# The prologue of a cross-attention and mixture-of-experts kernel: loads and constants in another order, keys ahead of queries, both first normalizations on VectorE

## The reference

```python
x = x + attention(layernorm(x), ctx)      # x, ctx: (8, 256, 256) f32
    q = layernorm(x) @ Wq + bq            # 16 heads of depth 16
    k, v = ctx @ Wk + bk, ctx @ Wv + bv
    attn = softmax(q @ k^T / 4 + mask * -1e9)   # mask: (8, 1, 1, 256)
    out = concat(attn @ v) @ Wo + bo
x = x + moe(layernorm(x))                 # 8 experts, top 2 of softmax(x @ w_gate),
                                          # capacity 1024, silu(a) * g @ c_proj
```

## Time and profile before

| what | value |
|---|---|
| runs | 487.96, 491.83, 487.74 us; median 487.96 |
| profiled execution | 487.79 us, its span 486.0 us |
| mean granted TensorE clock | 0.917 of full speed |
| busy: PE, DVE, POOL, ACT | 80%, 54%, 37%, 35% of the span |
| first row maximum on TensorE | 34.75 us after the span's start |
| start of the experts' steady part | about 300 us |

### The profile page before, as it was taken

How to read it: one execution, slowest core, us unless ns; L and a number is a source line. 1 busy time by engine, 2 the same in 40 slices (tenths; PEclk the granted TensorE clock), 3 DMA queues, 4 the chain that set the end, 5 groups by cost and what they waited for, 6 DMA issues and landing times.

```text
span 486.0 us, 8302 instructions
## 1 busy us (share of the span) xinstructions
PE 389.5 (80%) x2218; PEld 257.8 (53%) x2219; DVE 262.5 (54%) x684; ACT 171.9 (35%) x336; POOL 177.6 (37%) x179
## 2 busy tenths in 40 slices
PE   0647798996969979695868799679999999999970
PEld 0524455664645656453535466457666566656640
DVE  3638566686987969688687546223323232323220
ACT  1430638463654726453354252112221212121210
POOL 5542333322743717352213315213323232323231
PEclk9977889898988989798898689889999999999996
DMA  7499194938749193580405513533232333233420
GB/s 230 152 196 147 38 207 159 207 115 161 213 120 227 50 185 112 128 160 33 140 10 179 187 42 77 109 77 40 51 58 36 60 43 57 43 57 44 61 44 4
DMA packets 65430, 51.75 MB, mean 106 GB/s; under 512 B 11880, under 2 KB 62328, under 8 KB 65400
## 3 DMA queue, kind: packets, MB, share of 16 engines
q1 hardware_dynamic: 57224, 42.36, 38.0%
q0 software_dynamic: 7008, 8.43, 10.3%
q10 hardware_dynamic: 1168, 0.59, 0.5%
HBM read 32.89 MB, written 19.06 MB: 107 GB/s over the span
## 4 chain that ended last, share of the span: by engine, by line
DMA 31%; DVE 25%; PE 24%; issue 10%; SPq 4%; ACT 2%; POOL 1%; ACTq 1%; POOLq 1%; DVEq 0%
DMA out<-CTt,GG 26%; DVE NEG L1043 7%; PE bank L803 5%; PE bank L769 4%; PE bank L868 3%; PE bank L839 3%; PE bank L852 2%; PE bank L776 2%; DVE bn L1001 2%; PE bank L918 2%; DVE AVT L1062 2%; DMA wf<-qparts_d 1%; DVE AVN L1065 1%; DVE ON L1070 1%; DVE R L1079 1%
## 5 line engine op out<-in xcount | busy, mean ns | idle before, releaser
L918 PE MATMUL bank<-wf,XN 128*128 x304 | 108.1, 498 | 1.6 <-DVE CTt L1268 1.0
L571 POOL DMA_INDIRECT out<-CTt,GG x38 | 58.9, 1551 | 133.5 <-DMA out<-CTt,GG 108.5
L1043 DVE TENSOR_REDUCE NEG<-bank 128x2 f32<-128x512 f32 x128 | 83.4, 682 | 42.0 <-PE bank L839 41.2
L670 ACT ACTIVATE PR<-bank 128x512 f32<-128x512 f32 x128 | 73.0, 593 | 80.1 <-PE bank L852 68.6
L918 PEld LDWEIGHTS bank<-wf,XN 128*128 128x128 f32 x304 | 55.5, 194 | 34.7 <-issue 8.2
L839 PE MATMUL bank<-KS,wf 99*128 99x256 bf16 x256 | 52.0, 288 | 22.4 <-DVE NEG L1043 15.1
L1261 DVE TENSOR_TENSOR QF<-bank,KF 128x384 f32<-128x384 f32 x38 | 21.2, 557 | 73.3 <-PE bank L918 72.7
L711 ACT ACTIVATE XTt<-bank 128x384 f32<-128x384 f32 x38 | 18.7, 492 | 117.0 <-PE bank L931 117.0
L938 PE MATMUL bank<-wp,XTt 128*128 x228 | 58.3, 394 | 0.7 <-ACT XTt L711 0.7
L852 PE MATMUL bank<-wf,KS 102*128 102x256 bf16 x256 | 49.7, 278 | 6.0 <-ACT PR L670 5.6
L521 POOL DMA_INDIRECT slots<-R,slot x32 | 32.5, 1015 | 43.6 <-DVE slot L1146 32.0
(11 more groups left out here) (160 smaller groups left out, 503.3 us busy)
## 6 DMA issues: line engine op xcount, KB each, us to landing
wf<-in_L_ffn_c_fc SPq DMA_DIRECT2D x8, 768.0 KB, 6.2
XG<-slots SPq DMA_DIRECT2D x40, 128.0 KB, 2.7
kparts_d<-KP SPq DMA_DIRECT2D x8, 384.0 KB, 2.5
qparts_d<-QP SPq DMA_DIRECT2D x8, 384.0 KB, 2.6
KS<-kparts_d SPq DMA_DIRECT2D x8, 384.0 KB
KS<-kparts_d SPq DMA_DIRECT2D x24, 128.0 KB
wf<-qparts_d SPq DMA_DIRECT2D x8, 384.0 KB
wf<-qparts_d SPq DMA_DIRECT2D x24, 128.0 KB
```

The costliest lines, as they stand in the source:

```text
L571: pool.indirect_dma_start(out_rows, bass.IndirectOffsetOnAxis(ap=GG[:, u, 1:2].bitcast(U32), axis=0), Y[:, u, :], None, bounds_check=last_ ...
L670: act.activation(PR[:, s % NPROB, :], STB[s % 2][:], ACT.Exp).then_inc(exp_done, 1)
L918: ins = pe.matmul(bank[2 + 2 * u + g][:, 0:FF], XTG[:, u, k, :], wf[:, bass.ds(off + (k * 2 + g) * FF, FF)], start=k == 0, stop=k == KC - 1)
L1043: dve.tensor_reduce(NEG[:, n % 2, t, 2 * hp:2 * hp + 2], MXB[m % 2][:].rearrange("p (i s) -> p i s", i=2), AX.X, ALU.max, negate=True).the ...
```

## The change

Only the order and the place of work change; every value is computed as before.

- SyncE: the mask and X of sequence 0 are issued ahead of Wk; context 1 and X 1 follow the weights and biases of K and Q; Wv and bo are behind these. X 2 is issued between the row loads of sequences 0 and 1. Context 2, Wo, bv, w_gate and X 3 to 7 are issued behind the row loads of sequence 1. The semaphore for Wk, bk and Wv is split in two, and that of bo is taken from bq's.
- SyncE, sequences 0 and 1: the keys' rows are read back before the queries' parts are written. From sequence 2 on the order stays.
- `AT`: K moves from 3 to 1 and XT from 1 to 2, for all sequences; the second key part of sequences 0 and 1 to 2 (ahead of the evacuation of XT in the same unit), their second query part from 6 to 5. BO moves from unit 5 to 12 of iteration 0.
- GpSimd: of the 13 constants only `ident` and `mhalf` stay first; then `ones_rows(0)`, `layernorm1(0)` and the rest of the constants. `normalize1` of sequence 1 goes to VectorE; the memsets of slots 1 and 2 still wait for it.
- ScalarE: starts after two constants with one exponential of a single column.
- VectorE: the mask first; then statistics and normalization of sequence 0; both splits of sequence 0; statistics and normalization of sequence 1; then the memset of `VA` and the casts of the constants; then both splits of sequence 1; then the loop.

```diff
-    "X2 of the last": 10, "LG of the last": 11, "CNT": 1, "BO": 5,
-    "CT": 0, "XT": 1, "K": 3, "Q": 4,
-    "second K": 5, "second Q": 6,
+    "X2 of the last": 10, "LG of the last": 11, "CNT": 1, "BO": 12,
+    "CT": 0, "K": 1, "XT": 2, "Q": 4,
+    "second K": 5, "second Q": 6, "second K of the first": 2, "second Q of the first": 5,
...
-PROJECTION = ("CT", "XT", "K", "Q")
+PROJECTION = ("CT", "K", "XT", "Q")
...
+        def split_keys(eng, n):
+            first_rest(eng, n, KF, KP, KREST, kp0_ready, krest_ready, kp_ready)
+            last_part(eng, n, KP, KREST, kp1_ready, kp_ready)
+
+        def split_queries(eng, n):
+            first_rest(eng, n, QF, QP, QREST, qp0_ready, qrest_ready, qp_ready)
+            last_part(eng, n, QP, QREST, qp1_ready, qp_ready)
...
             load_context(0)
-            sp.dma_start(wk[:], Wk.rearrange("(k p) n -> p k n", p=P)).then_inc(wkv_in, 16)
-            sp.dma_start(X[:, 0:TB, :], x_t[0]).then_inc(x_in[0], 16)
-            sp.dma_start(bkc[:], bk.rearrange("(c p) -> p c", p=P), allow_slow_non_contiguous=True).then_inc(wkv_in, 16)
+            sp.dma_start(maskrow[:], mask.rearrange("b i j s -> b (i j s)")).then_inc(mask_in, 16)
+            load_rows(0)
+            sp.dma_start(wk[:], Wk.rearrange("(k p) n -> p k n", p=P)).then_inc(wk_in, 16)
+            sp.dma_start(bkc[:], bk.rearrange("(c p) -> p c", p=P), allow_slow_non_contiguous=True).then_inc(wk_in, 16)
             sp.dma_start(wq[:], Wq.rearrange("(k p) n -> p k n", p=P)).then_inc(wq_in, 16)
             sp.dma_start(bqc[:], bq.rearrange("(c p) -> p c", p=P), allow_slow_non_contiguous=True).then_inc(wq_in, 16)
-            sp.dma_start(maskrow[:], mask.rearrange("b i j s -> b (i j s)")).then_inc(mask_in, 16)
...
+            load_context(1)
+            load_rows(1)
+            sp.dma_start(wv[:], Wv.rearrange("(k p) n -> p k n", p=P)).then_inc(wv_in, 16)
+            sp.dma_start(bob[:], bo.partition_broadcast(P)).then_inc(bob_in, 16)
...
                 if it == -1:
+                    load_context(2)
                     load_rest()
+                    for n in range(3, B):
+                        load_rows(n)
...
+                    if n == 1:
+                        load_rows(2)
...
+                    write_parts(n, KP, kp_ready, kd_out, kparts_d)
+                    if n < 2:
+                        read_rows(n, KS, ROWS3, 0, MATCH_K, kd_out, kparts_d)
+                    write_parts(n, QP, qp_ready, qd_out, qparts_d)
+                    if n >= 2:
+                        read_rows(n, KS, ROWS3, 0, MATCH_K, kd_out, kparts_d)
+                    read_rows(n, QS, 0, ROWS3, MATCH_Q, qd_out, qparts_d)
...
+            const(pool.memset(mhalf[:], -0.5))
+            ones_rows(0)
             layernorm1(0)
-            ones_rows(0)
+            const(pool.memset(ones[:], 1.0))
...
                 if it == -2:
                     layernorm1(1)
-                    normalize1(pool, 1)
...
-            act.wait_ge(const_step, CONST_ALL)
+            act.wait_ge(const_step, CONST_IDENT)
+            act.activation(ex[:, 0, 0:1], ident[:, 0:1], ACT.Exp).then_inc(ex_warm, 1)
+            act.wait_ge(ex_warm, 1)
...
-            stats1_of(0)
-            normalize1(dve, 0)
-            dve.memset(VA[:, :, :, :, DH:32], 1.0).then_inc(va_ones, 1)
-            dve.memset(chosen[:, 0, 0, :], 0.0).then_inc(dve_const, 1)
             dve.wait_ge(mask_in, 16)
...
             dve.tensor_tensor(mparts[:, 2, :], mres2[:], mparts[:, 1, :], ALU.subtract).then_inc(mask_split, 1)
-            dve.wait_ge(wq_in, 48)
-            dve.tensor_scalar(bq4[:], bqc[:], 0.25, None, ALU.mult).then_inc(dve_const, 1)
+            dve.wait_ge(mask_split, 1)
+            stats1_of(0)
+            normalize1(dve, 0)
+            dve.wait_ge(wq_in, 32)
+            dve.tensor_scalar(bq4[:], bqc[:], 0.25, None, ALU.mult).then_inc(bq4_ready, 1)
+            split_keys(dve, 0)
+            split_queries(dve, 0)
+            stats1_of(1)
+            normalize1(dve, 1)
+            dve.memset(VA[:, :, :, :, DH:32], 1.0).then_inc(va_ones, 1)
+            dve.memset(chosen[:, 0, 0, :], 0.0).then_inc(dve_const, 1)
             dve.wait_ge(const_step, CONST_ALL)
...
             dve.wait_ge(dve_const, DVE_CONSTS)
-            dve.wait_ge(mask_split, 1)
+            split_keys(dve, 1)
+            split_queries(dve, 1)
...
             for it in ITERATIONS[:-1]:
-                if it == -1:
-                    split(dve, 0)
-                    split(dve, 1)
```

More of the change, by code:

```diff
@@ L284, in program @@
         CONST_ALL = 13
-        DVE_CONSTS = 10
+        DVE_CONSTS = 9
         def normalize1(eng, n):
@@ L356, in load_up, with write_parts, read_rows @@
                              c_fc[e].rearrange("(k p) f -> p k f", p=P)).then_inc(we_in, 16)
+            def write_parts(n, parts, ready, back, dram):
+                sp.wait_ge(ready, n + 1)
+                sp.dma_start(dram[n % 2].rearrange("c p j t -> p c (j t)"),
+                             parts[:].rearrange("p c j t -> p c (j t)")).then_inc(back[n % 2], 16)
+            def read_rows(n, dst, own, other, match, back, dram):
+                sp.wait_ge(back[n % 2], 16 * (n // 2 + 1))
+                sp.dma_start(dst[own:own + ROWS3, n % 3, :, :],
+                             dram[n % 2].rearrange("c (h d) j t -> (d j) (c h) t", d=DH)).then_inc(kq_in[n % 3], 16)
+                for j in range(3):
+                    sp.dma_start(dst[other + j:other + ROWS3:3, n % 3, :, :],
+                                 dram[n % 2][:, :, match[j]].rearrange("c (h d) t -> d (c h) t", d=DH)).then_inc(kq_in[n % 3], 16)
             late_after = {}
@@ L379, in _ @@
                                  mparts_d[n].unsqueeze(1).broadcast_to([3, H, S])).then_inc(kq_in[n % 3], 16)
[L381 to L394, removed]
+                    if n >= 2:
+                        sp.wait_ge(kq_in[(n - 2) % 3], KQ_LOADS * 16 * ((n - 2) // 3 + 1))
+                    write_parts(n, KP, kp_ready, kd_out, kparts_d)
+                    if n < 2:
+                        read_rows(n, KS, ROWS3, 0, MATCH_K, kd_out, kparts_d)
+                    write_parts(n, QP, qp_ready, qd_out, qparts_d)
+                    if n >= 2:
+                        read_rows(n, KS, ROWS3, 0, MATCH_K, kd_out, kparts_d)
+                    read_rows(n, QS, 0, ROWS3, MATCH_Q, qd_out, qparts_d)
                 if 0 <= it - 1:
@@ L470, in _ @@
             const.n = 0
[L471 to L480, removed]
-            const(pool.iota(iota_i[:, 136:136 + RESTBLK], [[1, RESTBLK]], base=0, channel_multiplier=0))
-            const(pool.iota(iota_i[:, 192:192 + RESTBLK // 2], [[2, RESTBLK // 2]], base=0, channel_multiplier=0))
-            const(pool.iota(tok_no[:], [[P, NT]], base=0, channel_multiplier=1))
-            const(pool.memset(pad_row[:, 0:D + 1], 0.0))
-            const(pool.iota(pad_row[:, D + 1:D + 2].bitcast(U32), [[0, 1]], base=PAD_TOK, channel_multiplier=0))
-            assert const.n == CONST_ALL
             def layernorm1(n):
@@ L660, in pad_tail @@
             def pad_tail():
+                act.wait_ge(const_step, CONST_ALL)
                 tail = slots[E * REGION:XROWS, :].rearrange("(n p) f -> p n f", p=P)
@@ L679, in _ @@
                 for u in range(UNITS):
-                    for n in projected_at(it, u, AT["second Q"]):
+                    for n in projected_at(it, u, AT["second Q of the first" if it == -2 else "second Q"]):
                         second_part(n, QP, QREST, qrest_ready, qd_out, qp1_ready)
@@ L683, in _ @@
                         exponentials(it, u)
-                    for n in projected_at(it, u, AT["second K"]):
+                    for n in projected_at(it, u, AT["second K of the first" if it == -2 else "second K"]):
                         second_part(n, KP, KREST, krest_ready, kd_out, kp1_ready)
@@ L762, in misc @@
                     if n == 0 and kind == "K":
-                        pe.wait_ge(wkv_in, 48)
+                        pe.wait_ge(wk_in, 32)
                     if n == 0 and kind == "Q":
-                        pe.wait_ge(wq_in, 48)
+                        pe.wait_ge(wq_in, 32)
                     dst = take_bank(kind, n)
@@ L772, in misc @@
                 elif kind == "V":
+                    if n == 0:
+                        pe.wait_ge(wv_in, 16)
                     dst = take_bank(kind, n)
@@ L1225, in _ @@
                         route_slots(it - 2)
-                    if u == AT["stats1"] and 1 <= it + 3 < B:
+                    if u == AT["stats1"] and 2 <= it + 3 < B:
                         stats1_of(it + 3)
@@ L1233, in _ @@
                         residual(it - 1)
-                    if u == 0 and it == 0:
+                    if u == AT["BO"] - 2 and it == 0:
                         bias_columns()
```

38 lines of the change are left out of this document (23 added, 15 removed).

## The result

The changed kernel takes 493.14 us (median), the kernel before beside it on the same chip 488.51. Its time over that of before is 1.0084, 95% interval 1.0057 to 1.0111: slower by 4.1 us (2.8 to 5.4), within 1% by its centre. The profiled execution has a span of 489.9 us at a mean granted clock of 0.913, where before had 486.0 at 0.917. The forecast was 492.8. All ratios here leave out, on both sides, executions more than 1.5% above the fastest of the same kernel, so a ratio can differ from that of the two medians.

A forecast was written before the change was run, and what follows sets the result against it. Before, the query rows' DMA held R, VectorE's first row-maxima reduction, at 35.39 us. Terms: 3.2 (R at 38.6, held casts) + 1.5 + 0.6 (K ahead of XT) - 0.3 (BO) = +5.0 on 487.8: 492.8 us, range 483 to 497.

The forecast's parts named there:

- K at 6.9, last query part at 19.2, or 20.3 with a slow projection: Sequence 0, prologue: K starts at about 6.9 us instead of 13.47; last query part ends at 19.2 instead of 22.00.
- Normalization of sequence 1 done at 22.4: VectorE, prologue: sequence 1's statistics and normalizations end at 22.4 us, against 22.14 on GpSimd before; worth nothing alone.
- Held casts: VectorE, prologue: constant casts blocked by GpSimd's four memsets until 30.4 us, first reduction 3.2 us later; as overall case, chance 0.55.
- Q of sequence 1 at 2.6 us (1.9 to 3.1): TensorE, prologue: sequence 1's query projection takes 2.6 us, after TensorE has idled about 7 us.
- K ahead of XT, sequence 2: +1.5: Iteration -1: Q waits for XT's evacuation behind ScalarE's key work, up to +1.85 us; +1.5 taken (0.3 to 1.9).
- K ahead of XT, steady state: +0.15 each, +0.6 in all: Sequences 4 to 7: Q about 0.3 us later, partly offset by GpSimd's earlier key split; range -1.5 to +2.0.
- An iteration's period changes by over 0.5 us: Sign that the prediction is wrong; from iteration 1 on it expected the period to change by less than 0.4 us.
- BO: -0.3 (-1.5 to 0): TensorE, iteration 0: moving BO's 1.60 us to unit 12, under the row maxima's DMA wait, gains 0.3 us.
- Edits at nothing: Early exponential, later loads of context 2 and X 3, and keys' read-back before queries' writing: all hidden, no effect.
- Rival D: Loads pushed too far back: context 2 over 2.6 us late or bk late stalls TensorE; 496 us, chance 0.15.
- The sum: Whole kernel: 3.2 + 1.5 + 0.6 - 0.3 = +5.0 us on 487.8, so 492.8 us.
- the intended gain: Prologue: earlier K and Q of sequence 0 let the DMA allow the first reduction at 28 to 30, some 5 to 7 us.

The follow-up runs named there:

- experiment 1: Changed kernel with VectorE's memset of `VA` and constant casts moved between the two splits of sequence 0: ratio 1.0008 to the kernel before, median 490.24 us.
- experiment 2: Changed kernel with GpSimd's memsets of slots 1 and 2 moved ahead of sequence 1's reciprocal deviation, without their wait: ratio 1.0015 to the kernel before, median 488.48 us.
- experiment 3: Changed kernel with the old order of XT and K for sequences 2 to 7, prologue as changed: ratio 1.0018 to the kernel before, median 490.45 us.
- experiment 8: Changed kernel with context 2 early, sequence 1's statistics, normalization and constants between sequence 0's splits, old order from sequence 1 on: ratio 0.9979, median 484.9 us.
- experiment 4: Changed kernel with sequence 1's second key part behind XT's evacuation on ScalarE: ratio 1.0064 to the kernel before, median 492.02 us.

## Why the prediction came out

The forecast was right in its time and in its main cause. One of its terms was far too small, and by one of its own signs of being wrong it was wrong. Here it is taken step by step.

- **K at 6.9, last query part at 19.2, or 20.3 with a slow projection.** K at 6.91, released by the landing of bk as said. It took 3.75 us, not 3.06, Q 2.50, and the last part ended at 20.27.
- **Normalization of sequence 1 done at 22.4.** 23.31, out of the 1.1 us of the line above. No gain by itself, as said.
- **Held casts.** Right, and shown by experiments 1 and 2 from both sides. The Trainium skill, "SBUF — State Buffer", "Who interferes with whom", stated both halves that the traces show: the casts are blocked (up to 1.90 us against 0.22), the subtraction of two SBUF inputs beside a memset, which only writes, is not (0.69). The size was off: I held one cast for each of four memsets and had the constants done at 30.4. Three memsets let all eight through, at 29.04, since casts that had started ended together with the one in front. The mask's first scaling was held as well, which I had not seen: at 3.81 us, beside a memset of slot 0, it took 1.72 us instead of 0.27. It had cover; the rows were normalized at 10.24, as forecast.
- **Q of sequence 1 at 2.6 us (1.9 to 3.1).** It took 3.78. The granted clock is 0.50 from 22 to 35 us, TensorE having waited 6.3 us ahead of it. That is above the range, by 0.7, and makes up for the line above: R at 38.32 against 38.6. The prediction's "2.5 to 4.3 with the two sizes of Q" is a slip: its own sum gives 2.5 to 3.7 with Q at 1.9 and 3.1.
- **K ahead of XT, sequence 2: +1.5.** R to L0 +1.2; with the old order it goes back (experiments 3 and 8: 18.47 and 18.50).
- **K ahead of XT, steady state: +0.15 each, +0.6 in all.** This is the step that failed, by size. Measured between context and Q: +0.54 in iteration 1 and +0.97 in each of iterations 2 to 4, 3.5 us in all; WO1 to WO5 without the output projections grew by 3.3. The ratio of the order alone says 2.0 us (-0.3 to 4.3), which holds all of these. I read the pattern from iteration 1, where Q starts 7.8 us after the transposes of context, and took it for the steady one. For that iteration the working was nearly right: XT's evacuation 8.1 us after the transposes, measured 8.25, and Q 0.3 later, measured 0.54. But in iterations 2 to 4 of the kernel before Q starts 6.8 us after the transposes, so there the same queue on ScalarE costs a full microsecond. I also left out that ScalarE's key work stands ahead of an exponential, that logits wait for that exponential's bank, and that Q stands behind the logits. That GpSimd's split of the keys starts earlier, for which I took 0.15 off, gave back nothing that the marks show. And sequence 3 had no term: in iteration 0, from context to Q takes 8.5 us instead of 7.2, though only 0.5 of that arrives at WO1. "An iteration's period changes by over 0.5 us" was one of my own conditions for being wrong, and it was met: from WO4 to WO5 it is 30.63 us instead of 28.79.
- **BO: -0.3 (-1.5 to 0).** +0.1, outside on the other side by a hair; nothing.
- **Edits at nothing.** Context 2 was just covered, and only while R was late: experiment 1 shows 1.3 us of wait for it with R at 35.66, near where it was before, experiment 4 shows 3.9 with R 4.8 us earlier than in the changed kernel. Rival D had the mechanism right and its condition wrong.
- **The sum.** +5.0 forecast. The marks give +6.5 up to WO8, the experts' part, untouched, came out 2.6 shorter in this one trace, and the timing says +4.1 (2.8 to 5.4). The time is right partly because errors cancel, and that part is luck: constants 1.3 us too late and Q 1.2 too short, and an order that costs 2.9 us more than I took between context and Q, against faster output projections and a shorter experts' part in this trace.

And the intended gain? The early K and Q are real: with memsets and casts apart, context 2 loaded in time and the old order kept (experiment 8), R comes at 31.60 and waits for a DMA, 3.8 us earlier than before. The forecast for that DMA was 28 to 30, "some 5 to 7 us"; in that run Q of sequence 0 took 3.78 us, and the last query part ended at 21.71 instead of 19.2. The change spends this and 2.9 us more on casts behind memsets and on a half-speed Q. But even kept, it is worth under 1% of this kernel.

## What to carry to other kernels

When work moves onto VectorE, look at what GpSimd does in the very same microseconds: constants that cost 0.2 us each cost what GpSimd's memsets last if both start at the same event, and it was this change's own wait that lined them up. When the order of two independent products is swapped, follow every consumer on the evacuating engine, also the work that only stands behind it in the queue, and do it in more than one iteration before calling a pattern steady. And before a step is made earlier, look up how much slack each load has against its new due time: an edit that gained 4.8 us at one mark gave most of it to a load that had always been just in time.

## What was not expected of the hardware

- Several VectorE instructions that wait behind one GpSimd memset end together with it: casts started at 25.25 and 25.38 end at 27.15 and 27.17, the memset at 27.06. So here the cost went by the number of memsets, not of casts: eight were through after three.
- One and the same projection of 8 matmuls takes 1.89 to 3.78 us in these traces. Q of sequence 1, with 6.3 us of wait ahead and a granted clock of 0.50 (1.2 GHz), took 3.78; in experiment 4, with 1.2 us of wait and a clock of 1.00 (2.4 GHz), 1.99. In the prologue R waits for all of it, and in the loop an output projection varies in the same way: the first one, behind the same 0.6 us of wait, took 3.54 us before and 2.00 in the changed kernel. The profile's clock doesn't cover all of it: K of sequence 0, at 6.91, took 3.75 us and Q of sequence 0 in experiment 8, at 14.29, took 3.78, both where the profile has 1.00. Why is open.
- On one chip, results of projections reached ScalarE and VectorE 1.8 us late in three iterations, with a pause of 1.58 us in the weight loads, in two different kernels. Its cause stays open.
